# A store of the first layer norm's output issued from SyncE's queue and not from GpSimd's

## What is computed

```
q, k, v, g = x@Wq, x@Wk, x@Wv, x@Wg
gk = log_sigmoid(x@Wgk1@Wgk2 + bgk2) / 16
S_t = diag(exp(gk_t)) S_{t-1} + k_t^T v_t ;  o_t = (q_t * scale) S_t     # 4 heads
o = rms(o) * g_norm_w * silu(g)
x1 = layernorm(x + o@Wo)
h = gelu(x1 @ fake_quant(W_fc)^T + b + lora)
y = layernorm(x1 + h @ fake_quant(W_proj)^T + b + lora)
```

## Time and profile before

| | us |
|---|---|
| median of two timed runs | 5185.7 |
| lowest and highest | 5121.13 and 5250.27 |
| the profiled execution, its own time | 5120.94 |
| its span on the slowest core (core 1) | 5119.4 |
| spans of the other cores | 5083.1 to 5115.4 |

### The profile page before, as it was taken

How to read it: one execution, slowest core, us unless ns; L and a number is a source line. 1 busy time by engine, 2 the same in 40 slices (tenths; PEclk the granted TensorE clock), 3 DMA queues, 4 the chain that set the end, 5 groups by cost and what they waited for, 6 DMA issues and landing times.

```text
span 5119.4 us, 41238 instructions; the slowest of 8 cores (5083.1 to 5119.4 us)
## 1 busy us (share of the span) xinstructions
PE 2922.2 (57%) x13392; PEld 1302.6 (25%) x13392; DVE 1455.6 (28%) x2709; ACT 806.4 (16%) x1517; POOL 237.6 (5%) x399
## 2 busy tenths in 40 slices
PE   0114454455455325545555556658567987788777
PEld 0002122222122112222222222223223433343333
DVE  1122443244334333433434343242421001110111
ACT  0000110211121002101210211211121122111211
POOL 1000000000000000000000000000000000000000
PEclk8557677677667667677677677778688988899888
DMA  9623112202210332033022102103033343334332
GB/s 111 107 78 104 51 58 86 97 13 91 93 52 34 112 150 76 15 116 112 13 93 89 60 30 81 72 30 137 13 112 132 114 148 140 130 109 150 138 132 91
DMA packets 107263, 456.63 MB, mean 89 GB/s; under 512 B 28065, under 2 KB 40369, under 8 KB 71202
## 3 DMA queue, kind: packets, MB, share of 16 engines
q0 software_dynamic: 81216, 302.69, 18.4%
q1 hardware_dynamic: 25842, 151.29, 8.5%
HBM read 411.99 MB, written 75.50 MB: 95 GB/s over the span
## 4 chain that ended last, share of the span: by engine, by line
PE 50%; DVE 17%; DMA 14%; issue 9%; ACT 6%; another core or an unknown queue 2%; DVEq 1%; ACTq 0%; POOL 0%; SPq 0%; POOLq 0%
PE po L999 9%; PE pq L968 9%; PE pr L872 5%; DMA x2f<-Wfc 5%; PE pq L654 4%; PE pq L636 4%; DMA x2f<-Wpj 2%; PE pq L605 2%; PE po L834 2%; DVE xT L859 2%; PE pq L589 2%; DVE qfp L446 2%; PE po L838 2%; DVE stats L398 1%
## 5 line engine op out<-in xcount | busy, mean ns | idle before, releaser
L968 PE MATMUL pq<-qf,meg 128*128 128x512 bf16 x2048 | 494.3, 385 | 10.8 <-DVE za L953 8.3
L999 PE MATMUL po<-meg 128*128 128x512 bf16 x2048 | 452.4, 379 | 7.6 <-DVE z2a L986 7.6
L636 PE MATMUL pq<-meg,xT 128*128 128x512 bf16 x1024 | 243.2, 402 | 286.1 <-DMA meg<-wv_s 285.2
L458 PE MATMUL pt<-id,qbf 128*128 128x128 bf16 x512 | 60.7, 292 | 517.8 <-DVE qbf L453 517.8
L872 PE MATMUL pr<-meg,xT 128*128 128x512 bf16 x1024 | 278.2, 439 | 69.7 <-DVE xT L859 69.7
L439 ACT ACTIVATE sgn<-x2f 128x512 bf16<-128x512 f32 x128 | 80.7, 630 | 1378.3 <-DMA x2f<-Wfc 726.6
L654 PE MATMUL pq<-meg,xT 128*128 128x512 bf16 x1024 | 246.7, 406 | 42.8 <-DMA meg<-wg_s 42.2
L968 PEld LDWEIGHTS pq<-qf,meg 128*128 128x128 bf16 x2048 | 201.6, 99 | 267.3 <-issue 35.2
L999 PEld LDWEIGHTS po<-meg 128*128 128x128 bf16 x2048 | 199.8, 98 | 251.1 <-issue 11.3
L976 ACT ACTIVATE meg<-pq,cols 128x512 bf16<-128x512 f32 x256 | 175.5, 687 | 305.3 <-PE pq L972 305.1
L834 PE MATMUL po<-St,diagd 128*128 128x512 bf16 x256 | 135.2, 528 | 153.2 <-DVE og L820 91.5
(11 more groups left out here) (189 smaller groups left out, 3746.4 us busy)
## 6 DMA issues: line engine op xcount, KB each, us to landing
x2f<-Wfc POOLq DMA_DIRECT2D x64, 512.0 KB, 4.1
x2f<-Wpj POOLq DMA_DIRECT2D x16, 2048.0 KB, 8.3
meg<-wfc_s SPq DMA_DIRECT2D x32, 1024.0 KB, 5.8
meg<-wfc_s POOLq DMA_DIRECT2D x32, 1024.0 KB, 9.5
meg<-wpj_s SPq DMA_DIRECT2D x32, 1024.0 KB, 4.8
meg<-wpj_s POOLq DMA_DIRECT2D x32, 1024.0 KB, 5.1
xtm<-xin SPq DMA_DIRECT2D x8, 2048.0 KB, 8.5
meg<-wv_s SPq DMA_DIRECT2D x16, 1024.0 KB, 5.0
```

What stands on the lines that cost most here:

```text
L458: (lambda e, kk=kk, pbuf=pbuf: e.transpose(out=pt[:, kk * 128:(kk + 1) * 128], in_=pbuf[:, kk * 128:(kk + 1) * 128], identity=id128[:]))
L636: ems.append(lambda e, pb=pb, wsl=wsl, rc=rc, kk=kk, j=j: e.matmul(out=pb[:], lhsT=xT[:, kk * 512 + j * 128:kk * 512 + (j + 1) * 128], rhs ...
L968: ems.append(lambda e, pb=pb, slot=slot, o4=o4, kk=kk: e.matmul(out=pb[:], lhsT=slot[:, o4 * 1024 + kk * 128:o4 * 1024 + (kk + 1) * 128], ...
L999: ems.append(lambda e, pb=pb, slot=slot, kk=kk: e.matmul(out=pb[:], lhsT=slot[:, kk * 128:(kk + 1) * 128], rhs=h1[:, kk * 512:(kk + 1) * 512],
```

## The change

The store of `x1c` in part A is issued by SP in place of POOL. Nothing else is changed: what is stored, from where and to where, and the semaphore it counts on stay as they are.

```diff
                     op1=ALU.mult), rd=["x1r", "cols"], wr=["x1bf%d" % (c % 2)])
-                P.dma("gpsimd", lambda e, t=t, c=c: e.dma_start(
+                P.dma("sync", lambda e, t=t, c=c: e.dma_start(
                     out=x1v[:, 4 * t + c, :], in_=x1c[:]), rd=["x1c"], wr=["x1_s"],
                     chan="x1st", append=True)
```

## The result

The changed kernel takes 1.0098 of the time before, with a 95% interval of 1.0069 to 1.0127. On the 5121 us of the profiled execution before, that is 50 us (35 to 65). The profiled execution of the changed kernel took 5167.8 us with a span of 5166.2, against 5120.9 and 5119.4. The plain medians go the other way (5183.1 of 21 executions now, 5228.8 of 20 before), because both kernels have executions that are up to 5% longer at a lower clock, and how many of them fall into a series is chance; the ratio leaves them out. The ratio lies within 2%, but clear of 1.

A forecast was written before the change was run, and what follows sets the result against it. The prediction took the kernel as a chain hopping between engines, with the xtm load's start on the critical path at seven boundaries: 7 x 5.3 = 37 us plus 4.3 extras, 5120.9 + 41 = 5162 us; range 5133 to 5225.

The forecast's parts named there:

- The hold: At each of seven tile boundaries, SP's store waits for x1c, so the xtm load issues 4.29 us later.
- The first guess of no cost: Stores of chunks 0 to 2 on SP cost nothing; relieving POOL of 32 issues, 17.4 us, gains nothing.
- One sign that I had named for being wrong: At the boundaries, the xtm load's landing growing by over 3 us would show the forecast wrong.
- I take 1.0: At each boundary, the store ahead in SP's queue lengthens the xtm load by 1.0 us (-0.5 to 2.9).
- the fourth, the transfer: Fourth part: chunk 3's 512 KB store, now ahead of xtm in SP's queue, delays that load by 1.0 us.
- the two extras at boundaries: Additions before tile 7, +2 us (0 to 4), for overlapping POOL loads, and before tile 1, +0.3 us net.
- The start of part B: Feed-forward start: wfc loads, held behind the store, run beside the qf load, which may land 2 us later (0 to 5).
- I work from 5120.9: Baseline choice: the profiled execution's 5120.9 us, 65 us below the median of two timings, 5185.7.
- A: Rival: at boundaries the store costs the load nothing; 3.8 us each, 27 us, 5148 us total; chance 0.18.
- B: Rival: store must land before the load's data flow; 7.2 us a boundary, 50 plus 5 to 10, 5178 us; chance 0.14.
- C: Rival: store lands at its worst, 9.1 us, before each boundary's load starts; 94 us, 5215 or 5219 us; chance 0.04.
- D: Rival: SP is not held by the waiting store and POOL's 17.4 us come off; 5103 to 5121 us; chance 0.04.

The follow-up runs named there:

- the ladder: Seven-gap sums of three kernels: xtm load waiting for x1c, both stores behind it, 95.8 us; x1c's store ahead instead, 103.8; changed kernel, x1T store beside too, 114.1.
- the run without the x1T store beside the load: Changed kernel, with the last chunk's x1T store put on SP behind the next tile's loads, x1c's store still ahead: 1.0072.
- the run with both stores behind: Changed kernel, but xtm load waits for x1c and the last chunk's x1c and x1T stores stand behind the next tile's loads on SP: 1.0074.
- the wait-alone run: Kernel before, all x1c stores left on POOL, but the xtm load also waits for x1c: 1.0116.
- the run with the store behind: Changed kernel, with chunk 3's x1c store put behind the next tile's xtm, Wq and Wk loads, except in the last tile: 1.0023.

## Why the prediction came out as it did

**The mechanism held.** SP's order puts the last store ahead of the xtm load, the load waits for x1c, and nothing behind it absorbs the delay. The hold: forecast 4.29 us, seen 4.16 in the timeline, of which 3.75 without the store's own issue. The first guess of no cost for chunks 0 to 2 and for POOL's relief is borne out by the run with these alone, 0.9993. TensorE's idle time before the transposes went from 2.80 to 10.63 on the slowest core, where I expected about 8. The sum of the eight waits for xtm grew by 38 us where I expected 35, but that nearness is luck: tile 0's wait happened to be 12 us shorter, and the seven that count grew by 50 on the slowest cores, 44.5 on the median. One sign that I had named for being wrong came true on the slowest core: the load's landing grew by 3.3 us (8.5 to 11.8), over the 3 that I allowed. The median of the eight cores grew by 2.1 (8.2 to 10.3).

**The store ahead in the queue.** The step "I take 1.0" was right for the store by itself, if a little high: between the ladder's first two rungs lie 8.0 us, 1.1 a boundary, of which 0.4 are the store's issue, counted in the hold. With the x1T store there as well, the same store costs 12.9.

**The step that failed is the fourth, the transfer: it weighed one neighbour of the load and there are two.** The prediction read the x1T store, spoke of what POOL waits for ahead of it, and never asked when it runs beside the load after the shift. Its issue did not move with the load: it hangs on x1bf, and so the load's later start slid the two together, from 7.1 us apart to 2.9, in two queues. That is the ladder's last rung, 10.3 us in seven, 1.5 each, which the sum put at nothing. The sum for the boundaries was 37 + 2.3 = 39.3; seen are 44.5. The miss is smaller than the term left out because the rest was put too high: 39.3 against the 34.2 that the run without the x1T store beside the load shows. Of the two extras at boundaries, the gap before tile 1 grew by 7.0 us and before tile 7 by 7.4 where the others grew by 5.9 to 6.2 (median core): some 1.0 and 1.3 more, against a forecast of 0.3 and 2.

**The start of part B** was put at +2 (0 to 5) and is +4.4. I looked for contention at the qf load; the trace shows it one step earlier, at the x1T store that the qf load waits for, 8.43 us where it was 2.52. The qf load itself lands in 5.1 us (median core) before and after. It is the same omission as at the boundaries: the x1T store beside loads that now start late.

**The reference.** The text forecast 41 us more than the profiled execution, and 50 were measured; the term left out is as large as that difference. But the point, 5162, was left beside a median of 5185.7 taken from two timings 129 us apart. Read against that median it says faster, and that is the wrong way round. The step at fault is "I work from 5120.9" without carrying the 65 us over to the point. The range, 5133 to 5225, held the profiled execution's 5167.8 and the median's 5183.1, though only its upper end was drawn with the 65 us in mind.

**The rivals.** A (27 us, the load unhurt) is what the run with both stores behind shows at the boundaries, 26.2, but it isn't what the change does. B's 50 us is the size that came, though not its reason: the store ahead costs 1.1 a boundary and not 2.9. C and D didn't happen. The fit from the Trainium skill, "DMA: Bandwidth & Descriptors", "Anatomy of one DMA — SWDGE (gpsimd) path", which gave by the prediction's estimate a landing of 7.5 us after the load's issue, is too fast for the rows: 8.6 to 10.9 us (median of a core) with the x1c store alone ahead, 9.8 to 11.9 with the x1T store beside it. What the same page of the Trainium skill says under "Issuing engines are not separate DMA queues", that DMAs of all engines interleave on the same 16 DMA engines, agrees with the wait-alone run: with the stores on POOL beside it a load on SP took 11.8 us to its transpose, with the stores behind it on SP 8.0.

What stays open: why the two stores together cost more than each alone, why one core of each pair is hit and its neighbour is not, and how much the norm's chain could still give if it were spread into the background work. None of these was tried.

## What to carry to other kernels

A store that waits for a late result must not be put in a queue ahead of a load that is ready earlier; look not at how busy the queue's engine is (SP was idle almost throughout) but at what is the next thing behind the store and who waits for that. When a transfer slides in time, list everything in other queues that doesn't slide with it and now overlaps it; here a store behind the load in the load's own queue did no harm, and one from another queue at the same moment did. And if a load's start is found on the path, cut the load into the pieces whose buffers come free early, before thinking about queues.

## What the hardware showed that I had not expected

A 2 MB load on SP's queue landed in 7.8 to 8.3 us (median of a core, all eight) in the run with the store behind, where the x1T store started beside it, late (7.1 us), and the x1c store behind it in its queue, and in 10.9 to 12.1 us when 768 KB of stores started within 3.3 us of it: 3 us more, where the same bytes as a further load in its queue cost 2.3 (by 3.1 us per MB in the prediction). The 256 KB store costs more than half of what the 512 KB one does: 5.4 against 8.0 us in seven where each is alone, 10.3 against 12.9 on top of the other. It writes rows of 256 bytes, the other rows of 4096, and it comes from another queue; whether either is the reason, no run here tells.

The moment of issue did not decide what a store costs the load. Issued 2.8 to 2.9 us behind it, the x1T store cost 10.3 us in seven from POOL's queue, and from SP's queue, behind the load, it landed only after the loads.
